# Biases of the decays: from ScalarE's exponentials to a second pass of GpSimd

## What is computed

```python
def step(S, inp):
    q_t, k_t, v_t, b_g, b_beta = inp
    S = S * jnp.exp(b_g)[..., None, None]
    kv = jnp.einsum('mbhk,mbhkv->mbhv', k_t, S)
    dv = (v_t[None] - kv) * b_beta[..., None]
    S = S + k_t[..., :, None] * dv[..., None, :]
    o_t = jnp.einsum('mbhk,mbhkv->mbhv', q_t, S)
    return (S, o_t)
...
o = jnp.einsum('tmbhv,hm->bthv', ys, mode_w)
o = o * gate
return o.reshape(B, T, H * DV) @ Wo
```

## Time and profile before

| what | value |
|---|---|
| time, median of 3 runs | 4371.86 us (4367.66 to 4394.44) |
| the profiled execution, its span | 4385.0 us (no other time is recorded for it) |
| of it recurrence | from about 370 to about 3,910 us |
| TensorE busy | 3813.9 us, 87% |
| VectorE busy | 3552.6 us, 81% |
| ScalarE busy | 2905.5 us, 66% |
| GpSimd busy | 380.0 us, 9% |

### The profile page before, as it was taken

The page is one execution under the profiler, slowest core; times in us unless marked ns, Lnnn a source line. Parts: engine busy times, 40 slices in busy tenths (PEclk is TensorE's granted clock), DMA queues, the critical chain, the costliest instruction groups (busy, mean ns, idle before and its releaser), DMA issues. The chain is left out here.

```text
span 4385.0 us, 193447 instructions
## 1 busy us (share of the span) xinstructions
PE 3813.9 (87%) x85713; PEld 3121.1 (71%) x85713; DVE 3552.6 (81%) x6909; ACT 2905.5 (66%) x9768; POOL 380.0 (9%) x220
## 2 busy tenths in 40 slices
PE   5513898999999999998999899999998999979999
PEld 2203787788778878777877778777777787766666
DVE  5676898888889988888898889889898988835665
ACT  5743677777677777777776767777677777744443
POOL 1230010000001000000000001000000000000000
PEclk8756899999899999999999989999999999989999
DMA  4664122222222222222221222232222222121110
GB/s 115 166 173 118 49 57 76 57 57 62 70 57 57 69 69 60 62 53 68 57 66 48 75 57 57 59 77 65 53 58 68 66 56 61 45 67 32 34 34 8
DMA packets 311716, 289.21 MB, mean 66 GB/s; under 512 B 137816, under 2 KB 250336, under 8 KB 308832
## 3 DMA queue, kind: packets, MB, share of 16 engines
q1 hardware_dynamic: 310880, 276.83, 24.5%
HBM read 215.92 MB, written 60.82 MB: 63 GB/s over the span
## 5 line engine op out<-in xcount | busy, mean ns | idle before, releaser
L922 DVE TENSOR_TENSOR run_EL<-run_XL 128x30 f32<-128x30 f32 (+14 forms) x1920 | 643.4, 335 | 66.0
L923 DVE TENSOR_TENSOR run_XL<-run_XL,run_EL 128x30 f32<-128x30 f32 (+14 forms) x1920 | 637.3, 332 | 66.0
L1059 PE MATMUL run_SP<-run_KP 64*32 64x128 f32 x8192 | 581.4, 283 | 21.7 <-DVE run_KP L909 12.2
L992 POOL TENSOR_TENSOR run_DB<-run_DB,run_below 128x1024 f32<-128x1024 f32 x128 | 306.5, 2395 | 3213.9 <-DVE run_KP L909 1758.5
L795 ACT ACTIVATE run_DB<-run_DB,run_col 128x64 f32<-128x64 f32 x2048 | 541.4, 350 | 4.7 <-POOL run_DB L992 1.0
L885 DVE TENSOR_TENSOR run_SC<-run_SP,run_DB 128x512 f32<-128x512 f32 x512 | 341.0, 685 | 248.9 <-ACT run_DB L795 156.3
L1059 PEld LDWEIGHTS run_SP<-run_KP 64*32 64x32 f32 x8192 | 426.5, 111 | 94.5 <-issue 68.1
L802 ACT ACTIVATE run_KD<-run_PR,run_col 128x64 f32<-128x64 f32 x2048 | 481.9, 329 | 17.0 <-PE run_PR L1078 9.1
L808 ACT ACTIVATE run_R<-run_KS,run_col 128x64 f32<-128x64 f32 x1792 | 417.1, 325 | 83.2 <-PE run_KS L1086 83.0
L1063 PE MATMUL run_SP<-run_KP 64*32 64x64 f32 x8192 | 413.9, 231 | 8.6 <-issue 8.6
L815 ACT ACTIVATE run_Sdec<-run_S,run_decay 128x64 f32<-128x64 f32 x1536 | 416.3, 372 | 0.0
(11 more groups left out here) (200 smaller groups left out, 7523.7 us busy)
## 6 DMA issues: line engine op xcount, KB each, us to landing
run_DB<-G_s SPq DMA_DIRECT2D x512, 128.0 KB, 2.9
run_EG<-EG_s SPq DMA_DIRECT2D x128, 512.0 KB, 6.7
KQ_s<-proj_win SPq DMA_DIRECT2D x32, 768.0 KB, 7.5
run_win<-KQ_s SPq DMA_DIRECT2D x64, 384.0 KB
run_tab<-TAB_s SPq DMA_DIRECT2D x64, 256.0 KB, 7.0
run_V<-V_s SPq DMA_DIRECT2D x128, 128.0 KB, 3.1
V_s<-proj_vv SPq DMA_DIRECT2D x64, 128.0 KB, 3.1
TAB_s<-tab_tab SPq DMA_DIRECT2D x64, 128.0 KB, 2.4
```

The source lines that it names most:

```text
L922: v.link(dve.tensor_tensor(e, bcast(XL[:, r + 1:, r], 2, done), bcast(XL[:, r, 0:done], 1, rows), ALU.mult))
L923: less = dve.tensor_tensor(XL[:, r + 1:, 0:done], XL[:, r + 1:, 0:done], e, ALU.subtract)
L1059: pe.matmul(out[64 * e:64 * e + C, p].rearrange("p (z u) i -> p z (u i)", z=2), KP[f, key, p, t0:t1], KP[f, kq, p, t0:t0 + SPAN], start=Tr ...
```

## The change

ScalarE's exponential of a chunk becomes one instruction over all four pairs (128 x 4 x 64) without a bias. GpSimd gets a second instruction behind the mask of each half, which adds the biases, repeated along the 64 positions of a chunk; between the two stands a wait on a new semaphore, `masked`. GpSimd now waits for the load of `col`, and ScalarE's own wait for it moves from the exponentials to `keys_by_token`, the next reader.

```diff
--- before.py
+++ after.py
@@ -648,7 +648,7 @@
 
         (l_win, l_ga, l_gb, l_eg, l_col, l_v, l_tab, weighed, pe_t, act_t, rot_k, rot_q, pe_s, d_ready, d_exp, scored,
          dve_s, qd_done, xt_done, pe_kd, kd_done, pe_m, act_m, pe_r, act_r, pe_w, act_w, pe_f, act_f,
-         s_dec, pe_o, act_o, stored, l_const, lanes_done) = sems[:35]
+         s_dec, pe_o, act_o, stored, l_const, lanes_done, masked) = sems[:36]
         with nc.Block() as block:
             @block.sync
             def _(sp):
@@ -789,13 +789,11 @@
                 def exponential(n, c):
                     if c % GROUP == 0:
                         act.wait_ge(d_ready, 2 * n + 1 + c // GROUP)
+                    act.activation(DB[:, :, c, :], DB[:, :, c, :], ACT.Exp).then_inc(d_exp, 1)
+
+                def keys_by_token(n, c):
                     if c == 0:
                         act.wait_ge(l_col, 16 * (n + 1))
-                    for p in range(PAIRS):
-                        last = act.activation(DB[:, p, c, :], DB[:, p, c, :], ACT.Exp, bias=col[:, n % 3, 0, p, c:c + 1])
-                    last.then_inc(d_exp, 1)
-
-                def keys_by_token(n, c):
                     if c % 2 == 0:
                         act.wait_ge(pe_kd, GROUP * n + c // 2 + 1)
                     for p in range(PAIRS):
@@ -987,20 +985,23 @@
 
             @block.gpsimd
             def _(pool):
-                def only_below(half):
+                def only_below(n, half):
                     cs = slice(GROUP * half, GROUP * half + GROUP)
-                    pool.tensor_tensor(DB[:, :, cs, :], DB[:, :, cs, :], bcast(bcast(below[:, :], 1, GROUP), 1, PAIRS), ALU.add).then_inc(d_ready, 1)
+                    pool.tensor_tensor(DB[:, :, cs, :], DB[:, :, cs, :], bcast(bcast(below[:, :], 1, GROUP), 1, PAIRS), ALU.add).then_inc(masked, 1)
+                    pool.wait_ge(masked, 2 * n + half + 1)
+                    pool.tensor_tensor(DB[:, :, cs, :], DB[:, :, cs, :], bcast(col[:, n % 3, 0, :, cs], 3, SPAN), ALU.add).then_inc(d_ready, 1)
 
                 for n in range(NSEQ):
                     pool.wait_ge(l_ga, 64 * (n + 1))
+                    pool.wait_ge(l_col, 16 * (n + 1))
                     if n:
 
                         pool.wait_ge(rot_q, 2 * (n + 1))
-                    only_below(0)
+                    only_below(n, 0)
                     pool.wait_ge(l_gb, 64 * (n + 1))
                     if n:
                         pool.wait_ge(lanes_done, n)
-                    only_below(1)
+                    only_below(n, 1)
 
             @block.tensor
             def _(pe):
```

## The result

The changed kernel takes 4437.39 us in the median (4432.84 to 4439.04); the kernel before, on the same chip, took 4369.76 us (4359.01 to 4394.44). The ratio is 1.0138, with a 95% interval from 1.0105 to 1.017. It is slower by a little over one per cent. The profiled execution has a span of 4437.3 us against 4385.0, so 52.3 us are to be found. The medians lie further apart, 67.6 us, because the profiled execution of the kernel before was some 15 us longer than its median.

The account below looks back on a forecast made before the run. TensorE and ScalarE together were taken to set the pace, with some slack on VectorE. Terms -10, +4 and +59 gave +53 us, 4425 us on the 4372 median; own range 4396 to 4484, wide range 4295 to 4490.

Parts of the forecast that it names:

- The stall: VectorE's elimination: one instruction is held up beside GpSimd's new first-half pass, 2.03 us a turn, 126 us in 62 turns.
- Rival 2: Faster: VectorE is hardly held up, or TensorE and ScalarE gain more; -74 us, 4298 us; chance 0.20.
- The second half: The new pass beside a transpose and three score products, which read one operand from PSUM; nothing counted.
- rival 3: Much slower: the second half's new pass also holds up score products, 1 us more a turn, 4490 us; chance 0.08.
- ScalarE's part: A chunk's exponentials as one 0.52 us instruction, ready 0.54 us sooner; worth at most 1.2 us a turn on the path.
- this sign: VectorE's wait for exponentials should fall from 156 us to under 60 in turns at the full clock.
- The waits: VectorE's waits left in a turn: 0.2 us for exponentials, 1.45 for scores, 0.7 for rotated inputs.
- The clock: TensorE idles ahead of the merges and its clock falls: 3.8 us in a quarter of the turns, 59 us.
- Rival 1: The same sum with the clock as it is now: -6 us, 4366 us; chance 0.30.
- The ends: At the start four GpSimd passes fall on VectorE instead of two: +4 us; nothing counted behind the last turn.
- The sum: Whole kernel: -10 us in the turns, +4 at the start, +59 for the clock, +53 us on a span of 4385.

Follow-up runs that it names:

- e1: The changed kernel without GpSimd's second pass, the biases left out; 4307.55 us, ratio 0.9813 to the kernel before.
- e3: The changed kernel with only the second half's biases moved to GpSimd, the first half as before; 4382.31 us, ratio 0.9991 to the kernel before.
- e10: The changed kernel with 7 idle products added on TensorE behind the first merge; ratio 0.9878 to the kernel before.
- e9: The changed kernel again, unaltered, on another chip; ratio 1.02 to the kernel before.
- e8: The changed kernel with a third GpSimd pass, adding zeros, over the first half; 4665.18 us, ratio 1.0723 to the kernel before.
- e2: The changed kernel with GpSimd's second pass adding zeros and ScalarE keeping four exponentials with biases per chunk; 4474.98 us, ratio 1.02 to the kernel before.
- e6: The changed kernel with the first half's mask and biases summed a sequence ahead on GpSimd; 4305.48 us, ratio 0.9898 to the kernel before.

## Why the prediction was right, step by step

**The stall.** The mechanism was as forecast: one instruction of the elimination in each turn, the second or third, is nearly as long as the pass beside it. Its size was too high, 2.03 us a turn against 1.60 (51.59 - 49.99), because the pass itself is shorter: 1.90 us, not 2.4 to 2.6. The product is held for 1.78 us and loses 1.56 (less its own 0.22). The Trainium skill's rule (SBUF — State Buffer, SBUF: two separate sides), that the loser blocks for the whole instruction, agrees here: the product ends 0.07 us behind the pass. Rival 2 needed a stall under 1 us; e1, which has none, shows what it would have been: 0.9813, or 82 us on 4384, where the rival had 74.

**The second half costs nothing.** Right: e3 has no stall, and rival 3 falls.

**ScalarE's part.** The size of the gain, 1.2 us at the most, was right (e1: 1.00), and so was that the change would not keep it. The exponentials' 0.52 us were 0.42. Of the wait for exponentials the prediction wanted less than 60 us, in turns at the full clock; over the whole span 112.2 us are left, 103.3 of them in the 62 turns, and of these 86.9 in the 32 turns with a low stretch at the merges. The other 30 turns have 16.4, so this sign came true. In e10, where the clock is kept, it is 53.0.

**The waits.** Left over by the forecast were 0.2 + 1.45 + 0.7 = 2.35 us a turn, and 0.95 for the clock: 3.30. Measured: 3.42. The parts fit less well than the sum: 1.67 for exponentials, where 0.2 and the clock's 0.95 had been forecast, 1.35 for scores (1.45) and 0.41 for rotated inputs (0.7).

**The clock.** Right in kind: TensorE stands ready at the merges in 32 turns instead of one, the clock falls there in 32 turns instead of 22, and low time goes from 225 to 444 us. The two factors of the term were both off: a turn with a low stretch waits 2.2 us longer for exponentials than one without (86.9 / 32 against 16.4 / 30), not 3.8, and they are half of the turns, not a quarter. At e9's and e10's 0.32 us for each, the 219 us more are about 70 us, where the forecast had 59. The same figure comes near e8: 911 - 528 = 383 us more than in e9, or 2.0 us a turn, and 1.69 of stall make 3.7, where 3.24 was measured. This figure is one difference between two kernels (0.26 in the other pair), and the waits are not only the clock's. Rival 1, the clock as it was, falls.

**The ends.** The start was forecast at +4 us and came to +8: the first transpose of solved blocks ends at 453.9 us instead of 445.9. GpSimd's first pass waits for the biases' load until 381.79, where it began at 374.33, and the four passes then fall on four of VectorE's rotations, which take 2.81 to 3.25 us each: 3.3 us more than the two long ones before, near the forecast of 4. The forecast left out the stall in the first elimination, which lies ahead of the 62 turns (1.6 us); 2.4 us are a first rotation that starts 1.1 us later and a wait of 1.3 us for a table, and the rest is longer waits for scores.

Behind the last turn's elimination another 8.2 us were lost, for which the forecast had nothing. They are VectorE's waits, 17.2 us where it had 9.0. The rows point to the clock again: at the merges of the last turn it stood at 0.50 (the row from 3870.40 above), where it was 1.00 in the kernel before. No run tests this turn by itself.

**The sum.** 37 us in the turns and 8 at each end make 53, and the span grew by 52.3; the stage of the experts took about 1 us less. The forecast of 53 was made of -10, +4 and +59. It came out through errors that cancel: VectorE's work was forecast at 51.9 us and came to 51.59 (19 us in 62 turns too dear), its waits at 3.30 and came to 3.42 (7 us too little), and the start and the end were 4 and 8 us too cheap. That there is a stall and what it costs VectorE, and that the lower clock takes part of the time, is shown by the runs; that the total fits to a few microseconds is luck. On the medians it fits less well: 4425 was forecast and 4437.39 measured.

What stays open is why e2 lies above its range. Its stall is that of the changed kernel, and its waits of 4.07 us a turn were expected smaller. Low time was 348 us, and TensorE waited 70.0 us for residuals; which of the two held VectorE up was not told apart by a run. Its single turns speak for the second: the 31 with a low stretch take 56.80 us, no more than the 57.11 of the changed kernel, while the 31 others take 54.74, where the changed kernel has 52.78.

## What to carry to other kernels

Work that is free on an idle engine is priced by what runs beside it: look for which instructions of VectorE read two operands from SBUF under each pass of GpSimd, and lay the pass beside transposes or reads from PSUM (e3, e6), even if it must be done a turn earlier. An engine that was late and becomes early stands idle, and on TensorE this idle time weighed as much as the stall that made it or more (filling it gave back 2.47 us a turn in e10, where the stall is 1.67): count it among the costs of any change that makes VectorE the bound. A few products in such a gap can be worth more than the change itself, but only as many as fit into it (7 against 14).

## What was not expected of the hardware

GpSimd's addition is faster when the second operand is repeated along the innermost axis: 1.90 us for 128x1024 with the biases or with zeros (1.902 in e2), 2.38 with the mask and also with the full tile `MB` (2.38 in e6). The product from which the prediction scaled, 0.66 us for 256 columns, makes 2.64 times four; its time did not scale with the columns, or a product differs from an addition, which no run tells apart.

When two of GpSimd's passes and VectorE's instructions stand queued against each other, the engines alternate: in e8 each of the two added passes held up exactly one instruction, 1.78 and 1.95 us in the rows shown, and not the rest of the elimination. It is so in all 63 eliminations that have passes beside them.
